# Scores by query issued between the two pieces of the scores by key

## The reference

```python
xn = _layernorm(x)
# layer A, per batch and head (16 heads of width 8)
scores = einsum('bhqd,bhkd->bhqk', rope(q), rope(k)) / sqrt(8);  scores[causal] = min
outA = softmax(scores) @ v ... @ out_w.T + out_b
# layer B, for c in range(6)
q = ew[c,0] * (nodes[c-1] @ We[eq] + be[eq])      # k and v alike, from older nodes
o = mha(q, k, v, Wq[c], Wk[c], Wv[c], Wo[c])      # 8 heads of width 16, softmax over 1024 keys
nodes[c] = act_w[c] * o + q
return x + outA + _layernorm(nodes[5]) 
```

## Time and profile before

| | |
|---|---|
| median of 3 runs | 1558.84 us (1556.27 to 1561.48) |
| the profiled execution: its own time | 1554.55 us |
| the profiled execution: span of the core | 1552.8 us |
| PE / ACT / DVE busy, share of the span | 96% / 72% / 76% |
| granted TensorE clock, mean | 0.987 |

### The profile page before, as it was taken

How to read it: one execution, slowest core, us unless ns; L and a number is a source line. 1 busy time by engine, 2 the same in 40 slices (tenths; PEclk the granted TensorE clock), 3 DMA queues, 4 the chain that set the end, 5 groups by cost and what they waited for, 6 DMA issues and landing times.

```text
span 1552.8 us, 61746 instructions
## 1 busy us (share of the span) xinstructions
PE 1490.3 (96%) x27114; PEld 748.1 (48%) x27114; DVE 1186.0 (76%) x1207; ACT 1118.4 (72%) x2219; POOL 446.3 (29%) x930
## 2 busy tenths in 40 slices
PE   6999999999999999999999999999999999999994
PEld 4567777754444444444444444444444444444431
DVE  7767776688877878878788787787877878878782
ACT  3366666667777777777788776787778877777682
POOL 5321111533323322333223331333223322330110
PEclk9899999999999999999999999999999999999997
DMA  7131111334232232322323222232232232321202
GB/s 240 43 100 45 47 46 40 134 100 145 74 102 96 86 106 72 118 88 75 107 82 117 94 72 85 100 107 93 74 102 97 91 99 73 117 87 55 70 25 63
DMA packets 116078, 138.48 MB, mean 89 GB/s; under 512 B 14946, under 2 KB 90467, under 8 KB 115683
## 3 DMA queue, kind: packets, MB, share of 16 engines
q1 hardware_dynamic: 115810, 134.54, 26.8%
HBM read 65.04 MB, written 62.39 MB: 82 GB/s over the span
## 4 chain that ended last, share of the span: by engine, by line
PE 84%; DMA 5%; ACT 3%; issue 2%; DVE 2%; SPq 2%; POOL 1%; ACTq 0%; DVEq 0%; POOLq 0%
PE s L948 52%; PE cps L1039 24%; PE misc L948 7%; DMA ks<-dram_qk_b 4%; ACT probs L729 3%; SPq L407 1%; SPq L484 1%; PE misc L943 1%; DMA ctx_b<-dram_raw_b 0%; DVE fin L812 0%; DMA ks<-dram_qk_a 0%; POOL parts L553 0%; PE misc L1182 0%; DVE stats L793 0%; POOL xtok L612 0%
## 5 line engine op out<-in xcount | busy, mean ns | idle before, releaser
L905 DVE TENSOR_REDUCE neg_max<-s 128x1 f32<-128x1024 f32 (+7 forms) x1024 | 1122.0, 1106 | 324.9 <-PE s L948 281.3
L729 ACT ACTIVATE probs<-s 128x512 f32<-128x512 f32 x1792 | 975.3, 598 | 317.6 <-PE s L948 312.8
L948 PE MATMUL s<-qs,ks 99*32 99x512 bf16 (+2 forms) x7680 | 683.9, 373 | 2.6
L948 PE MATMUL s<-ks,qs 96*32 96x512 bf16 (+3 forms) x7680 | 604.7, 370 | 12.3 <-DMA ks<-dram_qk_b 9.5
L1039 PE MATMUL cps<-probs,vs 128*32 128x256 f32 (+1 forms) x7296 | 596.5, 375 | 0.3 <-ACT probs L729 0.3
L948 PEld LDWEIGHTS s<-qs,ks 99*32 99x32 bf16 x7680 | 225.5, 94 | 383.3 <-ACT probs L729 267.5
L1039 PEld LDWEIGHTS cps<-probs,vs 128*32 128x32 f32 x7296 | 245.2, 109 | 172.4 <-ACT probs L729 0.8
L948 PEld LDWEIGHTS s<-ks,qs 96*32 96x32 bf16 x7680 | 221.1, 97 | 111.3 <-DMA ks<-dram_qk_b 13.1
L585 POOL TENSOR_TENSOR mparts<-neg_max,zeros 128x8 bf16<-128x8 f32 x128 | 26.0, 203 | 856.7 <-DVE neg_max L905 856.4
L948 PE MATMUL s<-mask_k,ident_h 128*32 128x128 bf16 x1024 | 100.7, 220 | 0.0
L651 POOL TENSOR_TENSOR parts<-full,zeros 128x512 bf16<-128x512 f32 x48 | 61.4, 1280 | 77.6 <-ACT full L760 77.6
(11 more groups left out here) (122 smaller groups left out, 605.2 us busy)
## 6 DMA issues: line engine op xcount, KB each, us to landing
dram_qk_b<-parts SPq DMA_DIRECT2D x48, 384.0 KB, 3.3
qs<-dram_qk_b SPq DMA_DIRECT2D x96, 192.0 KB
ks<-dram_qk_b SPq DMA_DIRECT2D x96, 192.0 KB
dram_qk_b<-parts SPq DMA_DIRECT2D x48, 256.0 KB, 3.1
dram_raw_b<-csb SPq DMA_DIRECT2D x96, 128.0 KB, 4.4
dram_qk_b<-parts SPq DMA_DIRECT2D x48, 128.0 KB, 3.4
vsrc<-srcT SPq DMA_DIRECT2D x12, 512.0 KB, 3.4
ctx_b<-dram_raw_b SPq DMA_DIRECT2D x48, 128.0 KB
```

The lines of the kernel that those rows point to most:

```text
L729: nc.scalar.activation(buf[:, lo:hi], s2[bank][:, 0:hi - lo], ACT.Exp, scale=scale).then_inc(exp_done, 1)
L905: last = ve.tensor_reduce(neg_max[k % 2][:, t:t + 1], s1[n % 2][:, lo:hi], AX.X, ALU.max, negate=True)
L948: last = te.matmul(dst[c0:c0 + STRIP, :], lhsT[:, c0:c0 + STRIP], rhs, start=start, stop=stop, tile_position=(0, c0))
```

## The change

In each turn the second piece of the scores by key (and any further one) is issued after the scores by query instead of ahead of them. The code of a piece is moved into a function, `score_piece`; its waits, its operands and its bank are the same. No instruction is added or removed on any engine.

```diff
@@ phase(), in the loop over the turns
                         j = step_at(kind, which, i)
+                        rest = []
                         if j is not None:
...
                             if i == 0:
                                 pe.wait_ge(mrow_in[(k - 2) % RING], 16 * (2 * ph + (k - 2) // RING + 1))
-                            for n, (lo, hi) in enumerate(pieces(which, j)):
-                                x0 = piece_no(kind, k, j) + n
-                                bank = s2[x0 % 2]
-                                need(pe, exp_done, PIECES.before(kind, r) + x0 - 1)
...
-                                last.then_inc(s2_ready, 1)
+                            score_piece(kind, r, k, j, 0)
+                            rest = range(1, len(pieces(which, j)))
                         if kind != "T":
...
                             last.then_inc(s1_ready, 1)
+
+                        for n in rest:
+                            score_piece(kind, r, k, j, n)
```

More of the change, by code:

```diff
@@ L1125, in last_node, with score_piece @@
                     last.then_inc(fin_ps, 1)
+            def score_piece(kind, r, k, j, n):
+                which = kind_at(kind, k, 2)
+                q, ky = qs[(k - 2) % RING], ks[(k - 2) % RING]
+                lo, hi = pieces(which, j)[n]
+                x0 = piece_no(kind, k, j) + n
+                bank = s2[x0 % 2]
+                need(pe, exp_done, PIECES.before(kind, r) + x0 - 1)
+                for t, at, q0 in key_tiles(which, j):
+                    first, end = max(lo, at), min(hi, at + S - q0)
+                    if first >= end:
+                        continue
+                    diagonal = which == "A" and first == at
+                    last = mm_strips(bank[:, first - lo:end - lo], ky[0:KALL, t * 128:(t + 1) * 128],
+                                     q[0:KALL, q0 + first - at:q0 + end - at], stop=not diagonal)
+                    if diagonal:
+                        last = mm_strips(bank[:, at - lo:at - lo + 128], ident_h[:, :], mask_k[:, :],
+                                         start=False)
+                last.then_inc(s2_ready, 1)
             def phase(kind, r, c, b):
@@ L1133, in phase @@
                         j = step_at(kind, which, i)
+                        rest = []
                         if j is not None:
-                            q, ky = qs[(k - 2) % RING], ks[(k - 2) % RING]
                             if i == 0:
                                 pe.wait_ge(mrow_in[(k - 2) % RING], 16 * (2 * ph + (k - 2) // RING + 1))
-                            for n, (lo, hi) in enumerate(pieces(which, j)):
-                                x0 = piece_no(kind, k, j) + n
-                                bank = s2[x0 % 2]
-                                need(pe, exp_done, PIECES.before(kind, r) + x0 - 1)
[L1143 to L1152, removed]
-                                last.then_inc(s2_ready, 1)
+                            score_piece(kind, r, k, j, 0)
+                            rest = range(1, len(pieces(which, j)))
                         if kind != "T":
```

## The result

| | before | changed |
|---|---|---|
| median of 13 runs each, same chip | 1558.84 us (1553.93 to 1562.22) | 1546.97 us (1540.72 to 1553.43) |
| ratio, with its 95% interval | | 0.9926 [0.9908, 0.9943] |
| profiled execution: time, span | 1554.55, 1552.8 us | 1542.79, 1541.0 us |
| granted TensorE clock, mean | 0.987 | 0.980 |

The change makes the kernel about 12 us (0.7%) faster. The forecast was 33 us faster, 1526 us, so a good third of it arrived. I take it apart against the profiled executions: 33.2 us forecast, 11.8 measured, some 21.5 missing.

A forecast was written before the change was run, and what follows sets the result against it. PE and ScalarE waiting for each other were taken to bound layer B. Gains of 26 us (ten `BL` phases), 2.9 (`B0`) and 4.3 (`BE`) make 33 us: 1521.3 profiled, 1526 as median, range 1504 to 1552.

The forecast's parts named there:

- The turn: Plain turn in the middle of a layer B head: 1.30 us instead of 1.365, PE no longer waiting for ScalarE.
- Layer A: PE already at its own pace there: gain 0, with bounds of 3 us either way.
- (D): `BL` phase from (3,0) to the node, set by a chain of DMAs: gain 0.2 us a phase.
- (C): `BL` phase from (0,1) to (3,0): gain 1.5 us, two stalls of 0.19 behind ScalarE's copies staying.
- (E): `BL` phase from the node to the transpose of (7,3): gain 1.1 us, after stalls of 4 x 0.19 and 2 x 0.09.
- (F): From the transpose of (7,3) to (0,1) of the next phase: loss 0.2 us, second piece following the `ks` wait.
- `B0` and `BE`: Layer B phases counted apart from the ten `BL` phases: gains of 2.9 and 4.3 us.
- Nothing to be measured: Rival: waits at the node and the boundary take up what the turns give; 1558 us, chance 0.07.
- More than that: Rival: copies behind the extras cost nothing; 1512 us, or 1496 if both DMA chains gave way; chance 0.17.
- ScalarE becomes the bound: Rival: handover 0.2 us longer, turns of 1.34, about 0.6 gained a phase; 1551 us, chance 0.18.
- VectorE holds the second piece up: Rival: the second piece stands behind late maxima in most turns of layer B; about 1590 us, chance 0.05.
- Switches between operands cost: Rival: PE drains at each of four operand changes a turn, 0.17 us each; 1640 us, chance 0.03.

The follow-up runs named there:

- experiment 4: New order in layer A's phases alone, old order in layer B: 1563.3 us, 1.0013 of the kernel before.
- 8: Changed kernel with nodes at (4,6) and (5,0), four projections moved, the next phase's first load issued early: 1503.35 us, 0.9618 of the kernel before.
- 12: The kernel of 8 with the old order of the pieces: 1539.82 us, 0.984 of the kernel before.
- 2: Changed kernel with the two node extras one turn later, at (4,5) and (4,7): 1527.24 us, 0.9774 of the kernel before.
- 9: Changed kernel again, no edit, on the same chip as 10: 1550.53 us, 0.9906 of the kernel before.
- 10: Changed kernel with eight groups of unused matmuls ahead of the node's wait, same chip as 9: 1538.94 us, 0.9837 of the kernel before.
- experiment 5: Changed kernel with the three projections of turn 5 moved to turn 4: 1555.33 us, 0.9934 of the kernel before.
- 6: Changed kernel with the old order in turn 0 of the first head of each layer B phase: 1552.2 us, 0.9934 of the kernel before.
- 1: Changed kernel with eight groups of unused matmuls ahead of the node's wait: 1540.21 us, 0.9862 of the kernel before.

## Why the prediction was wrong, step by step

**The turn: right.** "PE goes at 1.30 a turn" (1.30 to 1.31), no drain at the four changes of operand. Four changes of operand a turn instead of three cost nothing that shows, so the rule on draining in "TensorEngine Tiling (Array Packing)" of the Trainium skill, section Tiling Modes, has nothing to act on here: equal tilings, no cost in the trace. ScalarE's and VectorE's spare time held. One sign failed without harm: late loads were to be left only behind a copy, and most of those left are in plain turns, ahead of the first piece, where they cost nothing. Layer A gave nothing (experiment 4, heads of 8.12 in both). Experiments 8 and 12 measure the turns' gain at 35 us.

**The node, (D): the step that failed.** I wrote that the chain "hangs on SyncE's loads of step 3, which wait for the last context of turn 0", and so gave it 0.2 a phase for a context that is done earlier. SyncE's timeline before the change shows otherwise:

```profile
830.44 0.46 SPq L469 DMA_DIRECT2D dram_raw_b<-csb  x1
...
834.84 0.56 SPq L433 DMA_DIRECT2D sums<-dram_raw_b  x1
835.44 0.81 SPq L484 DMA_DIRECT2D qs<-mrows  x1
836.30 2.48 SPq L439 DMA_DIRECT2D ctx_b<-dram_raw_b  x4
838.82 1.61 SPq L375 DMA_DIRECT2D dram_qk_b<-parts  x3
840.48 1.36 SPq L407 DMA_DIRECT2D qs<-dram_qk_b  x1
841.89 0.91 SPq L407 DMA_DIRECT2D ks<-dram_qk_b  x1
842.85 0.46 SPq L469 DMA_DIRECT2D dram_raw_b<-csb  x1
```

and after it:

```profile
1125.28 0.46 SPq L469 DMA_DIRECT2D dram_raw_b<-csb  x1
1129.59 0.56 SPq L433 DMA_DIRECT2D sums<-dram_raw_b  x1
1130.20 0.80 SPq L484 DMA_DIRECT2D qs<-mrows  x1
1131.04 2.49 SPq L439 DMA_DIRECT2D ctx_b<-dram_raw_b  x4
1133.57 1.68 SPq L375 DMA_DIRECT2D dram_qk_b<-parts  x3
1135.30 1.21 SPq L407 DMA_DIRECT2D qs<-dram_qk_b  x1
1136.55 0.75 SPq L407 DMA_DIRECT2D ks<-dram_qk_b  x1
1137.35 0.49 SPq L469 DMA_DIRECT2D dram_raw_b<-csb  x1
1137.89 1.44 SPq L448 DMA_DIRECT2D dram_rec_b<-sums  x1
```

From 834.84 on, up to the reciprocals' issue at 843.36, and from 1129.59 on, each issue begins where the one ahead ends. The loads of step 3 don't wait for PE, they wait for their turn in the queue. What holds the queue ahead of them is the landing of the DMA issued at (2,0): the next issue comes 4.4 and 4.3 us after it. SyncE's own waits show it, once a phase, before the change and after it:

```profile
SPq L475 <- DMA dram_raw_b<-csb: 43.0, 11, 4.4
```

```profile
SPq L475 <- DMA dram_raw_b<-csb: 41.6, 11, 3.9
```

From the issue at (2,0) to that of the reciprocals it is 12.92 before and 12.61 after; on to the node it is 26.98 before and 26.85 after on average over the ten phases, nearly fixed. So the chain is anchored at the start of step 2, eight turns earlier than I had it, and what PE wins in those turns too is handed back at the node. Eight turns are worth 0.51 (from the transpose of (2,3) to that of (3,3), 11.02 before, 10.51 after), and that is what D misses: it got 0.3 longer on average where 0.2 shorter was forecast, 5.0 us in ten phases. From the transpose of (3,3) to the node the mean went from 13.74 to 14.26. Experiments 2 and 8 move the node towards the end of this chain, and most of the waits go.

**The clock: not in the sum at all.** I priced a wait as its length. It also halves PE's clock behind it, not every time. That is the largest single part: 8.6 us from the traces, 11.6 on one chip in experiments 9 and 10. The kernel before shows one such stretch in its ten phases, behind its longest node wait, and so gave notice. The Trainium skill, "TensorE: Matmul & The Clock Gate", Part 1, says that "the default state is throttled, and activity releases the throttle"; the trace agrees, with 1.2 GHz for 3.4 us behind a wait of 2.2. I had not weighed that rule, though I forecast the waits to grow.

**The copies, (C) and (E): right in kind, in half of the places too small in size.** I had 0.19 behind each key or query projection and 0.09 behind a value projection. In the middle of a head it is about that: turns of 1.50 to 1.55 (values 1.42) for 1.30. Where the late piece is that of turn 0 of the next head it is about 0.3 (values 0.2). ScalarE after (1,5) in the changed kernel,

```profile
1120.84 0.68 ACT L760 ACTIVATE full<-misc,cur_bias 128x512 f32<-128x512 f32 x1
1121.41 1.09 ACT L729 ACTIVATE probs<-s 128x512 f32<-128x512 f32 x2
```

and PE:

```profile
1120.55 0.39 PE L948 MATMUL s<-qs,ks 99*32 99x512 bf16 x4
...
1122.15 0.40 PE L948 MATMUL s<-qs,ks 99*32 99x512 bf16 x4
```

That turn lasts 1.60, 0.30 more than a plain one. Why turn 0 is worse wasn't isolated; its first piece waits for a DMA as well. With experiment 5's placing a head is 0.08 shorter.

**The boundary, (F): right.** The loss is 0.36 in the phase shown and 0.12 on average, for 0.2; the wait for `ks` is 1.35 for the forecast 1.4. On average over the phases, those with the halved clock left out, C gained 1.2 for 1.5 and E 0.95 for 1.1, so C, E and F together miss 3.8 us in ten phases.

**`B0` and `BE`:** 1.7 and 3.6 gained, counted between transposes of (7,3), for 7.2 together: 1.9 missing. Another 1.5 is time ahead of layer B (1.0) and in the tail (0.5), for which I had nothing and no run shows a cause.

8.6 (clock) + 5.0 (D) + 3.8 (C, E, F) are 17.4 of the 18.0 us missing in the ten phases (996.73 before, 988.77 after, 26 forecast). With 1.9 and 1.5 that is 20.8 of the missing 21.5 us.

**The rivals.** "Nothing to be measured" named the right mechanism, the waits at node and boundary, but had them take all; with the clock behind them they took about 40% (5.0 + 8.6 of 33). "More than that", "ScalarE becomes the bound", "VectorE holds the second piece up" and "Switches between operands cost" did not occur: the loads behind VectorE are late by 8.7 us in 1000. The time, 1547, is near the 1551 of "ScalarE becomes the bound", but that rival wanted turns of 1.34, and they take 1.30. It lies in the wide range I gave, outside the 1515 to 1540 of my own case; that the range held it is luck, for the reason is one that no term of the sum had. (A slip in the rivals: 0.085 in 64 turns of 12 phases is 65 us, not 63, which makes the lower limit 1494 instead of 1496.)

## What to carry to other kernels

When a change speeds up the engine that bounds the kernel, list first the points where it already waits for a chain it does not drive, and follow each chain back, issue by issue, until a row begins later than the one ahead of it ends: only there is its anchor, and all that the engine wins behind the anchor comes back as a wait. Price a wait of TensorE of some 2 us with the clock behind it, not by its length alone. Then move the waiting work: the same edit was worth 12 us with the waits in place and 35 us with them gone.

## What the runs showed of the hardware

- The granted clock falls to 0.50 for 3.4 us at a time (in experiments 5 and 6 once for 6.8). In the changed kernel, waits of 2.03, 2.34 and 2.33 us at a node were followed by one, waits of 2.08, 2.45 and 2.23 weren't, so length alone does not decide in that range. Matmuls of no use in the wait (1.95 us of them) removed all such falls behind the nodes, in experiments 1 and 10. What decides within that range stays open.
- The runs of the changed kernel are spread along with the clock: 1540.7 to 1541.0 us at 0.982 and 0.983, 1548.6 at 0.976, 1553.4 at 0.975. One execution is up to 6 us off the median (before, 5).
- SyncE needs 0.4 to 0.9 us for most single DMAs of this kernel (1.2 to 1.4 for some) and 2.5 for a row of four. Behind the wait for a landing, the rows from 1129.59 to the issue of the reciprocals at 1137.89 follow without a gap: 8.3 us of a chain that no engine shows as busy.
